# The second self attention of a two-layer transformer: value products inside the attention steps, and the layer's tail in halves

## What is computed

```python
qkv = xn @ Wqkv + bqkv
for h, stride in enumerate([1, 1, 2, 2, 2, 2, 4, 4, 4, 4, 8, 8, 8, 8, 16, 16]):
    k_s, v_s = k[:, h, ::stride, :], v[:, h, ::stride, :]     # head size 8
    scores = q[:, h] @ k_s^T / sqrt(8)
    outs.append(softmax(scores) @ v_s)
attn_out = concat(outs) @ Wout + bout
h = layer_norm(xn + attn_out, gamma, beta)
ffn = relu(h @ W1 + b1) @ W2 + b2                             # hidden size 512
x = x + layer_norm(h + ffn, gamma, beta)
```

## Time and profile before

| | us |
|---|---|
| runs, median (lowest to highest) | 591.32 (591.24 to 591.88) |
| the profiled execution, its own time | 592.91 |
| span of that execution | 590.9 |
| TensorE busy | 529.3 |
| VectorE busy | 376.1 |
| ScalarE busy | 334.3 |
| GpSimd busy | 213.7 |
| mean granted TensorE clock | 0.945 of full |

### The profile page before, as it was taken

How to read it: one execution, slowest core, us unless ns; L and a number is a source line. 1 busy time by engine, 2 the same in 40 slices (tenths; PEclk the granted TensorE clock), 3 DMA queues, 4 the chain that set the end, 5 groups by cost and what they waited for, 6 DMA issues and landing times. The chain is left out here.

```text
span 590.9 us, 10213 instructions
## 1 busy us (share of the span) xinstructions
PE 529.3 (90%) x3367; PEld 370.6 (63%) x3367; DVE 376.1 (64%) x887; ACT 334.3 (57%) x759; POOL 213.7 (36%) x236
## 2 busy tenths in 40 slices
PE   3989998998799997999979999796899987999996
PEld 1556675676356655888855668362466654777774
DVE  3388878778367625566653177736567457788875
ACT  1566776776257725456536065121376445889883
POOL 2677821000345630665631900103002372354510
PEclk9999999999799998999998599797899987999998
DMA  5722300000000000444402000000200001112101
GB/s 183 199 70 71 91 15 1 2 1 1 2 2 1 1 2 12 167 125 131 127 16 54 1 2 0 0 1 10 63 1 3 0 2 37 36 42 66 36 0 35
DMA packets 23456, 23.74 MB, mean 40 GB/s; under 512 B 3418, under 2 KB 17556, under 8 KB 23316
## 3 DMA queue, kind: packets, MB, share of 16 engines
q1 hardware_dynamic: 22560, 22.58, 13.2%
q10 hardware_dynamic: 852, 0.60, 0.4%
HBM read 22.56 MB, written 0.61 MB: 39 GB/s over the span
## 5 line engine op out<-in xcount | busy, mean ns | idle before, releaser
L1863 DVE TENSOR_TENSOR e_h_lo<-e_h,e_h_hi 128x512 fp32r<-128x512 f32 x60 | 47.8, 825 | 17.5 <-ACT e_h_hi L1724 17.4
L1128 POOL TENSOR_TENSOR e_gc<-e_g,e_c 128x512 f32<-128x512 f32 x32 | 41.9, 1312 | 42.1 <-ACT e_g L1111 22.8
L1720 ACT ACTIVATE e_h<-e_h,m_b 128x512 f32<-128x512 f32 x64 | 43.7, 688 | 10.9 <-PE e_h L1621 10.9
L544 ACT ACTIVATE a_p<-a_s,a_m 128x128 f32<-128x128 f32 x128 | 49.4, 390 | 0.0
L852 ACT ACTIVATE x_pT<-x_turn 77x1024 f32<-77x1024 f32 x32 | 32.5, 1017 | 17.9 <-PE x_turn L795 17.9
L1087 ACT ACTIVATE e_h_hi<-e_h 128x512 fp32r<-128x512 f32 x34 | 21.5, 632 | 34.3 <-DVE e_h L1170 26.1
L1176 DVE TENSOR_TENSOR e_h_lo<-e_h,e_h_hi 128x512 fp32r<-128x512 f32 x34 | 23.8, 699 | 26.0 <-ACT e_h_hi L1087 25.3
L1724 ACT ACTIVATE e_h_hi<-e_h 128x512 fp32r<-128x512 f32 x64 | 38.5, 631 | 0.0
L795 PE MATMUL x_turn<-consts,x_p 128*77 128x128 f32 x256 | 35.1, 281 | 1.8 <-ACT x_pT L852 1.8
L795 PEld LDWEIGHTS x_turn<-consts,x_p 128*77 128x77 f32 x256 | 29.1, 151 | 9.8 <-issue 7.3
L1762 POOL TENSOR_TENSOR m_w_hi<-m_w,e_one 128x512 fp32r<-128x512 f32 x16 | 19.0, 1186 | 43.2 <-PE e_y L1621 26.2
(11 more groups left out here) (301 smaller groups left out, 1459.0 us busy)
## 6 DMA issues: line engine op xcount, KB each, us to landing
e_c<-spread SPq DMA_DIRECT2D x32, 256.0 KB, 3.2
m_w<-in_L_ffn_W SPq DMA_DIRECT2D x16, 256.0 KB, 3.1
a_raw<-in_experts SPq DMA_DIRECT2D x17, 192.0 KB, 2.4
a_wkv<-in_L_attn_Wkv SPq DMA_DIRECT2D x2, 512.0 KB, 6.4
a_reversed<-scratch SPq DMA_DIRECT2D x4, 256.0 KB, 5.4
a_pick_f<-in_pick SPq DMA_DIRECT2D x1, 768.0 KB
x_all<-in_x SPq DMA_DIRECT2D x2, 256.0 KB, 5.3
a_wq<-in_L_attn_Wq SPq DMA_DIRECT2D x1, 512.0 KB, 6.5
```

The costliest lines, as they stand in the source:

```text
L544: done = act.activation(p[g % 3][:, h, :], s[g % 3][:, h, :], ACT.Exp, bias=m[g % 3][:, h:h + 1], accum_out=r[g % 3][:, h:h + 1])
L1128: pool.tensor_tensor(gc[k % 2][:, :], g[u % 2][:, :], c[k % NC][:, :], ALU.mult).then_inc(S["weighted"], 1)
L1720: act.activation(h[half][f], hb[f][:, :], ACT.Gelu, bias=b1[j][:, f:f + 1]).then_inc(S["gelu_done"], 1)
L1863: dve.tensor_tensor(h_lo[half][f][:, :], h[half][f], h_hi[half][f][:, :].bitcast(F32), ALU.subtract).then_inc(S["lo_done"], 1)
```

## The change

- The value products of a batch become four matmuls inside its second step (`values`, into free columns of score bank 1), and VectorE masks them right after that step's subtraction (`values_out`).
- Half 0's strided inputs are copied by VectorE at the start (`REPEATED`), half 1's by ScalarE in steps 2 and 4. GpSimd starts the keys of the first half when its K is out.
- There is no hardware loop: 16 steps are written out. Scores use two banks instead of four, the transposes follow the scores by one step, the products with the values by two.
- Half 0's tail stands in the steps: transposes of o after step 11, projection after step 12, its addition and statistics on VectorE in step 12, its scaling on GpSimd, transposes of h after step 15, and the up product before the last output product. gamma and beta of h go into ScalarE's copy of the transposed h (two more columns of `cols`).
- Half 1 follows, with down(0) beside it. The second norm of each half is followed at once by statistics, rstd, scaling and transposes for the next stage, so that the block layer_norm("n4_") is gone. Additions of bout, beta and beta + b2 move from VectorE to GpSimd.
- Of the fillers 24 stay in the tail and 4 at the start; the ten after the value products, 16 before h and 12 of the norm block go.

```diff
-        layer_norm("n4_")
...
+    V_AT = 2 * P
+    OT0, HT0 = 11, 15
+
+    VALUES = [(0, 2, None, P), (2, 4, 0, P), (6, 4, P, P), (10, 6, 2 * P, 80)]
+    REPEATED = [(2, 2, 64, 0), (4, 4, 32, P), (4, 8, 16, 2 * P), (2, 16, 8, 2 * P + 64)]
...
-            sbk = [ps(f"score{j}") for j in range(4)]
+            sbk = [ps(f"score{j}") for j in range(2)]
+            spare = [ps(f"spare{j}") for j in range(2)]
...
+            o_bank, y_bank = [spare[0], tb_rows[0]], [spare[1], tb_rows[1]]
+            up_bank = [spare[1], spare[0], sbk[0], sbk[1]]
+            qk_bank = [sbk[0], sbk[1], spare[0], spare[1]]
...
+                def values(b):
+                    pe.wait_ge(S[f"xk{b // HB}_ready"], 4)
+                    if b >= 1:
+                        pe.wait_ge(S["v_out"], b)
+                    for h0, nh, at, n_rows in VALUES:
+                        lhs = xnT_all[:, P * b:P * b + P] if at is None else xk[:, b, at:at + n_rows]
+                        pe.matmul(sbk[1][0:n_rows, V_AT + DH * h0:V_AT + DH * (h0 + nh)], lhs,
+                                       wqkv[:, 2 * P + DH * h0:2 * P + DH * (h0 + nh)], start=True, stop=True)
+
+                def scores(n):
+                    b, g = divmod(n, 2)
+                    if n < 4:
+                        pe.wait_ge(S["qk_out"], 2 if n < 2 else 4)
+                    if n >= 2:
+                        pe.wait_ge(S["shifted"], n - 1)
+                    if g == 1:
+                        values(b)
+                    pe.wait_ge(S["kb_done"], len(CLASSES) * b + (len(GROUPS[0]) if g == 0 else len(CLASSES)))
+                    mm = pe.matmul(sbk[n % 2][:, 0:WIDTH[g]], q[:, P * b:P * b + P], kb[:, b, SPLIT * g:SPLIT * g + WIDTH[g]],
+                                   start=True, stop=True)
+                    mm.then_inc(S["scores_done"], 1)
...
+                def projected(h):
+                    pe.wait_ge(S["oT_out"], h + 1)
+                    for b in range(HB * h, HB * h + HB):
+                        mm = pe.matmul(y_bank[h][:, P * (b % HB):P * (b % HB) + P], oT[:, P * b:P * b + P], wout[:, :],
+                                       start=True, stop=True)
+                    mm.then_inc(S["y_done"], 1)
...
+                def up(h):
                     pe.wait_ge(S["hT_out"], h + 1)
+                    if h == 0:
+                        pe.wait_ge(S["with_y"], 1)
...
+                def next_turned(h):
+                    bank = tb_rows[1 - h]
+                    if h == 0:
+                        pe.wait_ge(S["with_y"], 2)
+                    else:
+                        pe.wait_ge(S["hT_out"], 2)
+                    for b in range(HB * h, HB * h + HB):
+                        pe.wait_ge(S["xn_done"], b + 1)
+                        mm = pe.transpose(bank[:, P * (b % HB):P * (b % HB) + P], xn_all[:, b, :], ident)
+                    mm.then_inc(S["xn_turned"], 1)
+
+                for n in range(STEPS + 2):
+                    if n < STEPS:
+                        scores(n)
+                    if 1 <= n <= STEPS:
+                        weights_turned(n - 1)
+                    if n >= 2:
+                        outputs(n - 2)
+                    if n == OT0:
+                        out_turned(0)
+                    if n == OT0 + 1:
+                        projected(0)
+                    if n == HT0:
+                        h_turned(0)
+                    if n == STEPS:
+                        pe.wait_ge(S["shifted"], STEPS)
+                        pe.wait_ge(S["v_out"], B)
+                        up(0)
+                out_turned(1)
+                projected(1)
+                down(0)
+                h_turned(1)
+                up(1)
+                down(1)
+                next_turned(0)
+                keep_busy(pe, sbk[0], tables, 24)
+                next_turned(1)
...
+                for n in range(STEPS + 1):
+                    if n < STEPS:
+                        exponentials(n)
+                    if n >= 1:
+                        weights_out(n - 1)
+                    if n in (2, 4):
+                        repeated(1, REPEATED[n - 2:n])
+                    if n == OT0:
+                        out_out(0)
+                    if n == HT0:
+                        h_out(0)
...
+                relu(0)
+                out_out(1)
+                h_out(1)
+                relu(1)
...
+                for b in range(B):
+                    pool.wait_ge(S["qk_out"], 2 * (b // HB) + 1)
...
+                    if b == HB + 1:
+                        pool.tensor_tensor(halves(xn_all)[0], halves(xn_all)[0], row(bout), ALU.add).then_inc(S["x_ready"], 1)
+                pool.tensor_tensor(halves(xn_all)[1], halves(xn_all)[1], row(bout), ALU.add).then_inc(S["x_ready"], 1)
+                for h in range(2):
+                    pool.tensor_tensor(halves(x_all)[h], halves(x_all)[h], row(beta), ALU.add).then_inc(S["x_ready"], 1)
...
+                rstd_of(1, 0)
+                pool.wait_ge(S["rstd_ready"], 1)
+                for b in range(HB):
+                    ins = pool.tensor_scalar(hh[:, b, :], y[:, b, :], mv[:, b, 0:1], rstd[:, b:b + 1], ALU.subtract, ALU.mult)
+                ins.then_inc(S["h_ready"], 1)
+                h_scaled(0)
+                rstd_of(2, 1)
+                h_scaled(1)
+                for k, h in ((3, 0), (4, 0), (5, 1), (6, 1)):
+                    rstd_of(k, h)
...
+                for reps, stride, keys, at in REPEATED:
+                    dve.tensor_copy(free(xk[:, 0, at:at + 1], [[XK, HB], [keys, reps], [1, keys]]),
+                                    free(xnT_all[:, 0:1], [[P, HB], [0, reps], [stride, keys]])).then_inc(S["xk0_ready"], 1)
+                own_values(dve.memset(vm[:, :, :, :], 0.0))
+                own_values(dve.tensor_copy(vm[:, :, :, DH], free(own, [[0, B], [1, H]])))
...
+                def values_out(b):
+                    dve.wait_ge(S["scores_done"], 2 * b + 2)
+                    for n_rows, h0, h1 in ((P, 0, 10), (80, 10, 16)):
+                        src = sbk[1][0:n_rows, V_AT + DH * h0:V_AT + DH * h1].rearrange("p (h d) -> p h d", d=DH)
+                        ins = dve.tensor_tensor(vm[0:n_rows, b, h0:h1, 0:DH], src,
+                                                free(own[0:n_rows, h0:h1], [[1, h1 - h0], [0, DH]]), ALU.mult)
+                    ins.then_inc(S["v_out"], 1)
...
+                def with_down(h):
                     dve.wait_ge(S["down_done"], h + 1)
-                    own_values(dve.tensor_tensor(ys[h], pv[h][:, :].rearrange("p (b d) -> p b d", d=P), ns[h], ALU.add))
-                    norm(2 + h, h)
-                    own_values(dve.tensor_tensor(xs[h], xs[h], ys[h], ALU.add))
+                    dve.wait_ge(S["h_scaled"], h + 1)
+                    own_values(dve.tensor_tensor(ys[h], ob_rows[h], halves(xn_all)[h], ALU.add))
+                    statistics(y, h)
+                    own_values(*[dve.scalar_tensor_tensor(out=y[:, b, :], in0=y[:, b, :], scalar=mv[:, b, 0:1], in1=gamma,
+                                                          op0=ALU.subtract, op1=ALU.mult) for b in range(HB * h, HB * h + HB)])
+                    dve.wait_ge(S["rstd_ready"], 2 * h + 3)
+                    dve.wait_ge(S["x_ready"], 4)
+                    own_values(*[dve.scalar_tensor_tensor(out=x_all[:, b, :], in0=y[:, b, :], scalar=rstd[:, b:b + 1],
+                                                          in1=x_all[:, b, :], op0=ALU.mult, op1=ALU.add)
+                                 for b in range(HB * h, HB * h + HB)])
+                    statistics(x_all, h)
+
+                def next_norm(h):
+                    dve.wait_ge(S["rstd_ready"], 2 * h + 4)
+                    for b in range(HB * h, HB * h + HB):
+                        dve.tensor_scalar(xn_all[:, b, :], x_all[:, b, :], mv[:, b, 0:1], rstd[:, b:b + 1],
+                                          ALU.subtract, ALU.mult).then_inc(S["xn_done"], 1)
+
+                for n in range(STEPS + 3):
+                    if n < STEPS:
+                        shift(n)
+                        if n % 2 == 1:
+                            values_out(n // 2)
+                    if n >= 4 and n % 2 == 0:
+                        normalised(n // 2 - 2)
+                    if n == OT0 + 1:
+                        with_y(0)
+                with_y(1)
+                dve.wait_ge(S["rstd_ready"], 2)
+                for b in range(HB, B):
+                    ins = dve.tensor_scalar(hh[:, b, :], y[:, b, :], mv[:, b, 0:1], rstd[:, b:b + 1], ALU.subtract, ALU.mult)
+                ins.then_inc(S["h_ready"], 1)
+                with_down(0)
+                next_norm(0)
+                with_down(1)
+                next_norm(1)
...
```

(17 more changed lines are left out.)

316 lines of the change are left out of this document (115 added, 201 removed).

## The result

The changed kernel took a median of 574.63 us (571.17 to 578.45, four runs) against 591.28 (589.86 to 591.88, four runs) for the kernel before on the same chip: ratio 0.972, 95% interval 0.965 to 0.980, so 16.65 us faster. The forecast was 581.5 with a range of 569.5 to 590.5. The profiled execution took 571.17, its span 569.4; it is the fastest of the four.

What follows compares the result with a forecast made beforehand. Preparation was taken as bound by waits for copies, steps by TensorE, the tail by a chain through all engines. -17.1 + 15.5 - 19.0 = -20.6; +9.3 and +1.5 for the clock give -9.8: 581.5 us, range 569.5 to 590.5.

Steps and rivals of the forecast that it cites:

- Rival A: The forecast itself: TensorE's clock is lost in two to four batches, 578.4 to 584.6 us; chance 0.45.
- rival B: The clock holds in all steps: 570.7 us, with the slow start of the next stage 572.2; chance 0.28.
- Preparation: From the block's start to VectorE's first maximum: 5.6 us instead of 22.7, -17.1.
- Steps at full clock: First maximum to last reciprocal: 38.7 us of TensorE work plus 5.4 of waits and filling, 43.3 instead of 27.8, +15.5.
- Rival C: The clock holds, but the short lag costs 1.0 us of waiting a batch instead of 0.3: 577.8 us; chance 0.10.
- Half 0's tail in the steps: GpSimd's added operations stay hidden; half 0's h ready at 358.0, TensorE asks at 359.0, margin 1.0 us.
- Rival E: GpSimd hands h over late, steps 15 and on wait; 3 us of delay gives 574.2 us; chance 0.02.
- Tail: After the last reciprocal only half 1 is left: 25.8 us against 44.84, -19.0.
- The clock: Value products among the steps' scores lose TensorE's clock in three batches at 3.1 us each: +9.3, bounds 0 to about 25.
- The Trainium skill: Clock drops after idle gaps, so gapless steps stay full: -20.6 and up to +1.5; forecast set it against the trace.
- Rival D: Slower: clock lost in the first batches and not won back until the dense products, +7.6, 598.9 us; chance 0.10.
- The next stage's start: After a TensorE pause its four 512-column passes and fillers may run at half clock: +1.5 us, bounds 0 and 3.

Runs made afterwards that it cites:

- values_ahead: Changed kernel with all value products before the first scores again, second half's input copies also ahead of the steps: 581.57 us, ratio 0.979 to 0.986.
- keys_late: Changed kernel with GpSimd waiting for all four K and Q copies, not only the first half's K: 575.01 us, ratio 0.971 to 0.978.
- lag2: Changed kernel with transposes two and outputs three steps behind the scores, half 0's tail one step later: 574.33 us, ratio 0.967 to 0.976.
- after: The changed kernel itself, in its first profile: median 574.63 us, ratio 0.965 to 0.980; profiled execution 571.17.
- both_fill: fill35 plus five filler products on TensorE in step 14, where it stood 0.62 us: 570.06 us, ratio 0.961 to 0.967.
- fill35: Changed kernel with 35 instead of 24 fillers ahead of the second half's last transposes: 573.46 us, ratio 0.964 to 0.973.
- values_twice: Changed kernel with each value product in the steps issued twice: 577.67 us, ratio 0.975 to 0.981.
- all_fill: both_fill plus seven fillers in the tail's two TensorE pauses of 1.00 and 0.87 us: 565.69 us, ratio 0.955 to 0.962.
- half0_after: Changed kernel with the first half's tail (transposes, projection, norm, up product) behind the steps again: 577.97 us, ratio 0.971 to 0.981.
- banks4: half0_after with four score banks instead of two: 577.62 us, ratio 0.975 to 0.982.
- again: The changed kernel unedited, run once more for its spread and a second trace: 576.55 us, ratio 0.970 to 0.978.
- norm_block: Changed kernel with the next stage's norm as a block of its own, the fused one taken out: 575.64 us, ratio 0.971 to 0.979.
- ahead_lag2: Changed kernel with the edits of values_ahead and lag2 together: 579.68 us, ratio 0.978 to 0.988.

## Why the prediction was right, and where its steps failed

The total was right in sign and range, the likeliest value 6.9 us too high. Rival A as it was stated, 578.4 to 584.6, did not come; the median lies between it and rival B. In part the total is luck: the largest uncertain term, +9.3 for the clock, was charged for a reason that the runs refute. The 1.2 us that a measurement was to tell from no change was too small as well, since four runs of the changed kernel spread over 7.3. By its steps, in the section's own times:

**Preparation**: forecast 5.6, measured 5.51 in nearly every run. The working held term by term, GpSimd's early start among them. values_ahead shows what carries it: putting the value products back ahead of the scores, with their masks and the second half's copies, brings back 10.25 of the 17 us, keys_late gives 1.5 to the early keys; the rest I did not take apart.

**Steps at full clock**: forecast 43.3, measured 40.88 (keys_late). The term that was mis-sized is waits and pipe fill. TensorE was busy 38.68 of these 40.88 and idle 2.20; I had put 38.7 of work and 5.4 of waits into a stretch that begins 1.1 earlier (that sum gives 364.9, not the 365.1 that stands there; the 0.2 is in no term). In mid loop there is no wait at all (4.13 against 4.17 of work). Against that something that I had not costed: two batches of 4.77 and 4.36, behind ScalarE's copies of the second half's inputs (1.70 us from 320.45, 0.86 from 324.58), which stand between its exponentials. That the copies do it is argued: values_ahead, without them in the steps, has no such batch in mid loop, but it lacks the value products too. The short lag was judged well: "hidden by only 2.5 us of matmuls" is the coincidence that values_ahead and lag2 show from both sides. Rival C (1.0 of waiting a batch) did not come: TensorE has no wait in a mid-loop batch.

**Half 0's tail in the steps**: GpSimd's h came in time. In after its last scaling ended at 348.68 and TensorE took it at 349.75; in both_fill, at the full clock, 354.86 and 355.29, a margin of 0.4 where I had 1.0. Rival E did not come.

**Tail**: forecast 25.8 to the end of the last copy. fill35, at 1.00, has 26.33 to the next product, which starts 0.30 after such an end (387.54 and 387.84 in after): 26.0.

**The clock**: the size was off and the reason was wrong. I charged 9.3 us, three batches, because value products alone had run at 0.50, and called the mixture likely to lose it. values_twice refutes that: twice the value products, the clock at 1.00 for all 45.26 us. The cost was 4.3 in the steps and 1.7 in the tail of after, 6.0 in all. It hit the dense products behind the steps (up(0), 3 us) more than the batches. What the runs tie the losses to is TensorE waiting, and they do so unequally well:

- The 2.12 us before the last transposes. All nine profiles that have this wait fell to 0.50 within 2.1 us of its end; the three that have fillers there (fill35, both_fill, all_fill) did not fall before the next stage's first maximum.
- The 0.62 us at step 14 (0.59 in half0_after and banks4). Six of seven profiles with it fell at its very end or up to 3.0 us behind (from 348.4 in after, 354.0, 352.8 and 354.6 in again, fill35 and norm_block); keys_late did not. The three without it (both_fill, all_fill, values_twice) held 1.00 through the steps. values_ahead, lag2 and ahead_lag2, which stand longer near the end of the steps (1.40, 1.30 and 1.17 us), fell there too.
- The 1.00 and 0.87 us in the tail. Only three of ten profiles with them fell there (after, both_fill, ahead_lag2). That all_fill did not fall is little evidence for its seven fillers.

The trace of the kernel before had such rows too, which I did not use. Its clock fell at 375.61 and at 402.92, each time inside one of TensorE's two longest waits in the tail:

```profile
376.02 1.11 PE L1361 MATMUL b_turn<-consts,a_hh 128*128 128x128 f32 x4 [2.62 <-DVE a_hh L1530]
404.82 1.44 PE L96 MATMUL n_unread<-pick,ident_bf 96*128 96x512 bf16 x3 [3.73 <-PEq L1266]
```

A wait is not enough by itself, though. The first transposes of the steps come after a wait of 1.08 us in nine profiles, and none lost the clock in the 8 us behind it; the four waits of 0.71 us in values_ahead cost nothing either. The medians agree with the rest, but weakly (570.06 for both_fill against fill35's 573.46, with intervals that overlap a little). What makes one wait cost the clock and another not stays open. So does norm_block's loss at 392.1, inside the wait of 0.94 us that fill35 has without a loss, and again's at 330.1, where a wait of 0.23 us at 327.8 is the only one near.

**The Trainium skill** (TensorE: Matmul & The Clock Gate, section Why this matters for your kernels) was weighed and set aside: the clock drops after an idle gap between bursts. The section speaks of longer gaps than 2.12 us, so by its words none of the changed kernel's pauses should have cost the clock. The direction of the rule fits the steps and the next stage's start better than my reading of the earlier trace rows did, as the pause of 2.12 us and fill35 show. It does not cover itself, where the clock fell with TensorE busy 3.60 of 3.60 us; that row stays unexplained. The same page's Part 4 (PE-mode transpose), by which the steps would have fallen and stayed, is not borne out: steps with six transposes a batch held 1.00 throughout in four profiles. Rival D is refuted.

**The next stage's start**: forecast +1.5 within 0 to 3, measured +2.4 (after) to +2.65 (again). The mechanism was the one named, the pause before the last transposes.

**The sum**: -17.1 (forecast -17.1), +17.5 with the clock (forecast +15.5 and +9.3), -17.0 (-19.0), +2.4 (+1.5): -14.2 in the section, where I had -9.8. again has -14.1. Its medians, 14 to 17 us under before, agree with it as far as their scatter of 6 us goes. With the clock held by fillers (all_fill), against the kernel before as it ran, the change is worth 95.57 + 4.45 - 72.68 - 4.45 = 22.9 us in the section, where I had 20.6. Rival B's number, 570.7 to 572.2, is near what the change gives with two of TensorE's pauses filled (both_fill, 570.06).

## What to carry to other kernels

Work that sits ahead of a loop on the busy engine can go into the loop at almost no cost if the loop waits on a chain of other engines anyway; test that from both sides, once with the work out and once with it doubled, since two limits that coincide hide each other from any single experiment. When engines are made to overlap more, the pauses that remain on TensorE should be looked for one by one: filling the wait of 2.12 us won back 2.4 us at the next stage's start, and without the wait of 0.62 us none of three profiles had the loss of some 4 us in the steps. Such fillers cost nothing where the engine stood idle anyway (40.89 us of steps with them, 40.88 in keys_late without). With all fillers (all_fill) the median was 8.9 us below the changed kernel's, but not all of that is the fillers': where a loss comes and goes between profiles of one kernel, a single profile without it proves nothing.

## What the runs showed of the hardware

The place where TensorE's clock falls is not fixed for one program: again lost it at 330.1 and after did not. Ahead of the section, over the same unedited work, the profile of after ran at a mean of 0.99 and that of before at 0.97. Of the 6.75 us between the two profiled executions of the changed kernel (571.17 and 577.92) 5.3 lie ahead of the section. Filler products in a wait need not be counted exactly: 35 instead of 24 (7.72 us of them, to 389.51) ended while VectorE's last normalisations (388.77 to 389.88) were still running. And a stretch at 0.50 can outlast much real work: in half0_after it held for 20.40 us with TensorE busy for 15.01 of them. The same wait can cost the clock in one profile and not in the next: the 1.00 and 0.87 us in the tail did in three profiles of ten.
